# A three-layer graph network on one core: batch turns three tiles apart, sums in two buffers, edge weights ahead of z, edges begun one tile later

## The reference, cut to what matters

```
def gat_conv(x, src, dst, W, att_src, att_dst, bias, n):      # layers 1 and 2
    h = x @ W
    e = leaky_relu((h @ att_src)[src] + (h @ att_dst)[dst], 0.2)
    e = exp(e - segment_max(e, dst, n)[dst])
    alpha = e / segment_sum(e, dst, n)[dst]
    return segment_sum(alpha[:, None] * h[src], dst, n) + bias

def gcn_conv(x, W, b, src, dst, n):                           # layers 3 and 4
    h = x @ W
    norm = dinv[src] * dinv[dst]                              # dinv = 1/sqrt(degree)
    return segment_sum(h[src] * norm[:, None], dst, n) + b

h  = relu(layernorm(x))
x1 = x + gat_conv(relu(gat_conv(h, ...)), ...)                # src, dst with a self-loop per node
h  = relu(layernorm(x1))
out = x1 + gcn_conv(relu(gcn_conv(h, ...)), ...)
```

## Time and profile before

| | us |
|---|---|
| runs | 2162.92, 2172.12, 2168.01 |
| median | 2168.01 |
| profiled execution | 2162.72 |
| its span, first to last instruction | 2160.5 |
| TensorE busy | 2103.2 (97%) |
| VectorE busy | 1418.8 (66%) |
| ScalarE busy | 951.1 (44%) |
| POOL busy | 851.6 (39%) |
| granted TensorE clock, mean | 0.991 |

### The profile page before, as it was taken

How to read it: one execution, slowest core, us unless ns; L and a number is a source line. 1 busy time by engine, 2 the same in 40 slices (tenths; PEclk the granted TensorE clock), 3 DMA queues, 4 the chain that set the end, 5 groups by cost and what they waited for, 6 DMA issues and landing times.

```text
span 2160.5 us, 34890 instructions
## 1 busy us (share of the span) xinstructions
PE 2103.2 (97%) x12917; PEld 1312.5 (61%) x12917; DVE 1418.8 (66%) x3186; ACT 951.1 (44%) x1328; POOL 851.6 (39%) x1067
## 2 busy tenths in 40 slices
PE   7999999999999999999998999999998999999997
PEld 4666666556666666666665556666665666656664
DVE  8989754435776675435897888565466547876652
ACT  4444454434554554444554454333333343334442
POOL 3221167614332321344544443443344422336552
PEclk9999999999999999999999999999999999999999
DMA  5998899994555559998786443576797626776552
GB/s 185 237 223 200 229 216 195 214 233 161 192 176 196 197 180 245 230 219 217 261 282 214 166 161 132 165 248 223 265 318 281 226 103 213 245 223 215 196 193 93
DMA packets 297486, 451.94 MB, mean 209 GB/s; under 512 B 193267, under 2 KB 193465, under 8 KB 297190
## 3 DMA queue, kind: packets, MB, share of 16 engines
q1 hardware_dynamic: 256950, 277.12, 46.0%
q0 software_dynamic: 40368, 172.60, 25.5%
HBM read 234.94 MB, written 179.89 MB: 192 GB/s over the span
## 4 chain that ended last, share of the span: by engine, by line
PE 86%; DVE 6%; DMA 3%; ACT 2%; issue 2%; POOL 1%; SPq 0%; POOLq 0%; ACTq 0%; DVEq 0%
PE ps_h L1077 67%; PE ps_h L1096 9%; PE ps_z L1040 4%; PE ps_e L1175 1%; PE ps_e L1176 1%; PE ps_e L1165 1%; PE ps_e L1166 1%; DMA rows<-e_out 1%; DVE edge_mem L1393 1%; DVE bn L1264 1%; DVE x_keep L1290 0%; DVE x_keep L1286 0%; DMA edge_mem<-meta_rows 0%; DMA out<-res,perm_out 0%; DVE res L1382 0%
## 5 line engine op out<-in xcount | busy, mean ns | idle before, releaser
L1077 PE MATMUL ps_h<-w_hi,x_keep 128*128 128x384 f16 x2568 | 526.4, 326 | 1.1 <-issue 1.1
L1077 PE MATMUL ps_h<-w_hi,z_hi 128*128 128x384 f16 x1572 | 388.0, 329 | 1.5 <-DVE w_lo L1254 1.5
L1077 PE MATMUL ps_h<-w_lo,z_hi 128*128 128x384 f16 x1572 | 387.4, 328 | 0.0
L1077 PE MATMUL ps_h<-w_hi,z_lo 128*128 128x384 f16 x1572 | 386.4, 328 | 0.0
L1077 PEld LDWEIGHTS ps_h<-w_hi,x_keep 128*128 128x128 f16 x2568 | 249.9, 98 | 164.7 <-issue 2.4
L1077 PE MATMUL ps_h<-w_lo,x_keep 128*128 128x384 f16 x1284 | 313.7, 326 | 0.0
L903 ACT ACTIVATE row_out<-ps_h,grow 128x768 f32<-128x768 f32 x159 | 142.9, 899 | 366.8 <-PE ps_h L1077 365.9
L1330 DVE TENSOR_TENSOR z_lo<-ps_z,z_hi 128x768 f16<-128x768 f32 x131 | 125.0, 954 | 155.5 <-ACT z_hi L916 155.4
L734 POOL TENSOR_SCALAR veps<-mv 128x1 f32<-128x1 f32 x158 | 43.8, 277 | 458.0 <-DVE mv L1267 455.5
L1361 DVE TENSOR_TENSOR res<-z,res 128x768 f16<-128x768 f32 x107 | 102.3, 956 | 183.7 <-ACT res L949 94.3
L1077 PEld LDWEIGHTS ps_h<-w_lo,z_hi 128*128 128x128 f16 x1572 | 154.9, 99 | 104.1 <-issue 3.6
(11 more groups left out here) (252 smaller groups left out, 3609.9 us busy)
## 6 DMA issues: line engine op xcount, KB each, us to landing
rows<-row_out SPq DMA_DIRECT2D x199, 384.0 KB, 3.8
rows<-e_out SPq DMA_DIRECT2D x60, 384.0 KB, 4.6
row_in<-in_x SPq DMA_DIRECT2D x40, 384.0 KB, 4.3
row_in<-rows SPq DMA_DIRECT2D x40, 384.0 KB, 5.1
x_rows<-pre SPq DMA_DIRECT2D x40, 384.0 KB, 3.7
res<-x_rows SPq DMA_DIRECT2D x40, 384.0 KB, 4.4
pure_rows<-row_out SPq DMA_DIRECT2D x39, 384.0 KB, 2.6
row_in<-pure_rows SPq DMA_DIRECT2D x39, 384.0 KB, 4.9
```

The costliest lines, as they stand in the source:

```text
L1077: last = nc.tensor.matmul(ps_h[s][:, a, 0:HALF], zp[:, c, :], wp[:, c, a * HALF:(a + 1) * HALF], start=(c == 0 and zp is zh and wp is hi), ...
```

## The change

Four edits:

1. The three tiles of a batch that follows plain tiles (the first of each part: places 178, 248 and 286) are turned three places apart, at g - 7, g - 4 and g - 1 instead of g - 3, g - 2 and g - 1. In the other batches nothing changes.
2. The plain sums of layer 3 are written to two buffers by turns (`e_tmp` and `e_out`, as `last_out`), each with a semaphore of its own for its store; VectorE waits for the store before the last one. SP issues the store at the start of its window instead of at its end.
3. On ScalarE, `weights` comes before `make_z` instead of after it, in all score tiles of both layers.
4. The edges of layer 2 begin at place 161 instead of 160, the plain sums at 233 instead of 232. Their first gathers on POOL stay (`edge_rows(layer, 0)` at place 159) or move with them (the plain sums').

```diff
     def put_batch():
         b, g = count[0], len(seq)
         count[0] += 1
-        follows = b > 0 and seq[g - 1].chain
-        last = [t.g for t in seq if t.chain and t.layer == 4][-THREE:]
-        turns = [last[0], last[1], g - 1] if last and b > 0 and last[1] >= g - 12 else [g - 3, g - 2, g - 1]
+        apart = 1 if seq[g - 1].chain else 3
+        turns = [g - 1 - 2 * apart, g - 1 - apart, g - 1]
...
-    EDGES = {1: begin["2"] + 2, 2: begin["3"] + 2}
-    plain_at = {begin["4"] + 4 + (7 * j) // 5: j for j in range(ET)}
+    EDGES = {1: begin["2"] + 2, 2: begin["3"] + 3}
+    plain_at = {begin["4"] + 5 + (7 * j) // 5: j for j in range(ET)}
...
             def edge_store(layer, h, j):
-                if layer in GATS:
-                    sp.wait_ge(e_out_ready, h + 1)
-                else:
-                    sp.wait_ge(edge_done, h + 3)
+                sp.wait_ge(e_out_ready, h + 1)
                 sp.dma_start(table_tile(layer, NT + j), e_out[:, :]).then_inc(e_stored, 16)
+
+            def plain_store(j):
+                sp.wait_ge(edge_done, 2 * ET + j + 3)
+                sp.dma_start(table_tile(3, NT + j), last_out[j % 2]).then_inc(plain_stored[j % 2], 16)
...
+                if w - 1 in plain_at:
+                    plain_store(plain_at[w - 1])
                 t = tile(w, -1)
                 if t and t.stored:
                     store(t)
...
-                if w - 1 in plain_at:
-                    j = plain_at[w - 1]
-                    edge_store(3, j + 2 * ET, j)
...
                     if t.mixed and t.pos == FREE:
-                        pool.wait_ge(e_stored, 16 * ((t.layer - 1) * ET + 1))
+                        if t.layer == 4:
+                            for s in range(2):
+                                pool.wait_ge(plain_stored[s], (ET + 1 - s) // 2 * 16)
+                        else:
+                            pool.wait_ge(e_stored, 16 * ((t.layer - 1) * ET + 1))
...
                 for t in turned[:1]:
                     upper_parts(t)
+                if gat and not first and now is not None:
+                    weights(now + h0)
                 for t in due(w + 1):
                     make_z(t)
...
                     divide(before + h0)
-                if gat and not first and now is not None:
-                    weights(now + h0)
...
                 else:
-                    dve.wait_ge(e_stored, (h + 1) * 16)
-                    base = last_base[j % 4]
-                    V.tensor_tensor(e_out[:, 0:SPLIT], base[:, 0:SPLIT], e_lo, ALU.add)
-                    V.tensor_tensor(e_out[:, SPLIT:D], base[:, SPLIT:D], ps_e[:, 1, 0:D - SPLIT], ALU.add).then_inc(edge_done, 1)
+                    if j < 2:
+                        dve.wait_ge(e_stored, (2 * ET + 1) * 16)
+                    else:
+                        dve.wait_ge(plain_stored[j % 2], (j // 2) * 16)
+                    base, to = last_base[j % 4], last_out[j % 2]
+                    V.tensor_tensor(to[:, 0:SPLIT], base[:, 0:SPLIT], e_lo, ALU.add)
+                    V.tensor_tensor(to[:, SPLIT:D], base[:, SPLIT:D], ps_e[:, 1, 0:D - SPLIT], ALU.add).then_inc(edge_done, 1)
```

More of the change, by code:

```diff
@@ L501, in build @@
         e_stored = sem("e_stored")
+        plain_stored = [sem(f"plain_stored{s}") for s in range(2)]
         base_stored = [sem(f"base_stored{s}") for s in range(3)]
```

## The result

The changed kernel takes 2176.51 us in the median of 18 runs (2171.10 to 2182.19), the kernel before, on the same chips, 2167.38 (18 runs, 2160.36 to 2172.12). The ratio is 1.0044 with a 95% interval of 1.0035 to 1.0054: 9.5 us slower, between 7.6 and 11.7. The forecast was 2170.2 us, +2.2. The profiled execution took 2178.17 us, its span is 2176.0.

A forecast was written before the change was run, and what follows sets the result against it. TensorE, busy 97% of the span, was taken as the bound, so only its waits and lower clock could change; the terms summed to +2.2 us, put on the median of 2168.0: 2170.2 us, range 2155 to 2183.

The forecast's parts named there:

- E: Places 244 to 246: two sum buffers and turns three tiles apart would take 9.9 us off an excess of 10.4.
- F: Places 283 and 284: turns three tiles apart would take 3.3 us off an excess of 5.4.
- C: Four batches from place 178: edges from 161 make stripe 2 and product 1 late score tiles, +16.1 us.
- B: Places 173 to 176, before the first batch: spread turns find no room on VectorE, +3.6 us on 10.9.
- D: Place 234: two buffers for the third layer's sums would remove its whole excess, -2.8 us.
- A: Places 161 and 162, where the second layer's edges begin: starting one tile later takes 1.5 us off 4.7.
- Rival 1: VectorE's idle time absorbs the parity, so B and C would be 0: 2150.5 us, faster; chance 0.17.
- Rival 2: Lateness is carried from batch to batch, with four clock drops: sum +14.6, 2182.6 us, slower; chance 0.15.
- Rival 3: The sums' store did not hold E; its wait goes to the batch's low half: E -3, 2177 us; chance 0.06.

The follow-up runs named there:

- e3: The changed kernel with z put back ahead of the weights on ScalarE, edges still from place 161: 2178.32 us, ratio 1.0035 to the kernel before.
- e5: e4 with the turns three tiles apart in the first batch of the first part only: 2162.33 us, ratio 0.9979 to the kernel before.
- e9: e4 with the edges of layer 2 begun at place 161 instead of 160: 2177.60 us, ratio 1.0033 to the kernel before.
- e4: The kernel before with only the two buffers for the third layer's sums and SP's earlier issue of their store: 2159.40 us, ratio 0.9954.
- e1: The changed kernel with the edges of layer 2 begun at place 160 again: 2168.88 us, ratio 0.9985 to the kernel before.
- e2: The changed kernel with the edges of layer 2 begun at place 162: 2167.48 us, ratio 0.9988 to the kernel before.
- e8: e4 with turns three apart before the middle part only and the carried row ahead of the batch tile's z: 2153.88 us, ratio 0.9935.
- e7: e6 with POOL's factors for that batch's tiles computed after the next place's gather: 2152.37 us, ratio 0.9937 to the kernel before.
- e10: e4 with the weights ahead of z on ScalarE, edges from place 160: 2161.48 us, ratio 0.9960 to the kernel before.
- e6: e4 with the turns three apart before the last part only (before place 286): 2156.13 us, ratio 0.9946 to the kernel before.

## Why the prediction was right, and where not

The forecast of no change within 0.5% held; the size was 7 us short. In the traces the terms together miss by 8.9, of which E and F are 8.4. By its steps:

1. **C, parity: right.** +14.6 for +16.1. Stripe 2 was put at 1.8 us, measured 1.8 in each batch; product 1 at 3.2, measured 3.0 at a full clock (3.6 in the two batches where the clock fell within the place); two clock drops of four were put at 3.4, and two came, of 1.6 and 1.4 with the 0.6 that falls into product 1. Inside, one term was wrong: 0.8 us of each wait was laid on z behind the weights. With z first (e3), z waits for POOL's factors and the weights for z, and stripe 2 still has 1.9 and product 1 2.6 at a full clock: z behind the weights is worth nothing at the one and 0.4 at the other, and the rest belongs to the parity. VectorE's chain was put at 1.0 and 2.4, so at stripe 2 it was too short by as much as z was too long. That the sum came out there is luck.
2. **B: near in the sum, partly by luck.** Waits were put at 3.5 in place 170, 4.9 at the end of 171, and 1.3 + 2.2 in 174, the clock at 1.6 after 171 and about 1 for another drop; excesses of 3.2 (170), 5.1 (171), 1.7 (172), 3.9 (174) and 1.5 (175) came. But TensorE stood only 2.7, 3.2 and 1.1 + 2.2, and the clock fell three times: it is 0.88 in place 171, 0.80 in 172 and 0.84 in 175, which costs 1.6 + 1.7 + 1.5. The waits were put 2.7 too long and the clock some 2 too cheap. The prediction laid the rise on the spread turns alone (+3.6). Alone they make +5.0 (e5), the parity alone +4.3 (e9), both +5.2: the two do not add here (that they fill the same idle time of VectorE was not shown), and the term was some 1.6 small.
3. **D, two buffers: right**, -2.8 (e4), with the earlier issue in it.
4. **E: wrong by 3.9 us.** The -9.9 was to come from buffers and spread turns together. The buffers alone bring -8.3 (e4), and the changed kernel then has 2.3 more: place 240 has an excess of 3.8, the rest of E 0.6. 1.7 of the 3.8 is the clock; in e1, with the same wait of 1.89, it stays at 1.00, place 240 has 2.1 and E 2.7. In the four kernels with the same code here (it, e1, e2, e3) E is between 2.7 and 5.1. The sums also begin one place later in all four, and no run has that start alone, or these turns in this order without it. The failed step is "A batch tile's two loads move with it": it moved the loads, but not the batch tile's z on ScalarE, which waits for POOL's factors and now stands ahead of a carried row; with the row ahead of z, 0.6 is left (e8).
5. **F: wrong by 4.5 us, and in sign.** The same step ends in "the eviction that needs it comes two tiles, 13 us, later: 0". It followed SP's queue and asked only for the store; on POOL, factors and gather share one queue, and the rows of a plain tile came 1.3 and 2.1 us late. VectorE's balance (4.05 us over three places) was right: e7, which takes POOL's order away, leaves 1.8 where 2.2 were forecast. How late the rows come varies: in the four kernels with the changed kernel's order (it, e1, e2, e3) F is between 5.7 and 9.3.
6. **A: right**, -1.1 for -1.5.

Rival 1, that VectorE's idle time absorbs the parity, is refuted by e1 and e9. The share that it argued from even fell: VectorE was busy for 37.73 of 43.99 us of a batch and is for 38.65 of 48.32 now, 80% after 86, while TensorE waits more for it. The Trainium skill's "Perfetto Trace Analysis", section "Identifying the Most-Contended Engine", takes VectorE's occupancy as a fair measure of how close it is to roofline. It does not say that an engine with time to spare is never late; that reading, which the prediction gave as the page's, does not hold here. The work between an edge part and the next score is serial, and its lateness does not show in the share. Rival 2, lateness carried on, is refuted by the changed kernel's trace: the waits at product 1 are 2.6 us in the first batch and 2.5 in the three others, and two drops came, not four. Rival 3 is refuted by e4: E loses 8.3 with no turn moved.

The net of 9.5 us therefore comes from four edits. One gains (buffers with the earlier store, -10 us by e4), one loses more (edges at an odd place, +17 by e9), and one does next to nothing (weights before z, e3 and e10). The spread turns lose 5.0 in the first place by e5, where VectorE has no room, and 2.3 in the second, with the sums' later start in it; in the third, 0.6 (e6) is less than F varies from kernel to kernel. Added up, -10, +17, +5.0, +2.3 and +0.6 make 15: some 4 of it is counted twice, since in B the parity and the spread turns do not add. When the carried row and the gather go first, the spread turns gain 1.5 in the second place (e8) and 3.7 in the third (e7).

## What to carry to other kernels

An order that alternates with period two against a pattern of six has a phase; shift one against the other and a different step meets the longest chain, so the start place is a parameter to be tried at both parities. When a step is moved, write down its instruction on every engine, not only its loads: here the losses that the prediction missed came from a z and a gather that it had not counted. A second buffer and an earlier issue took away a wait on a store with no loss seen elsewhere; apply such an edit by itself, and each half of it by itself, before those that trade one wait for another.

## What the runs showed that was not expected

Layer 1, the same in all these kernels, had 2.9 us of excess in the profiled execution of before, and between 6.8 and 13.2 in the other twelve, mostly in places 61 to 70. The stretch in the changed kernel, and in the one before:

```profile
395.00:460.00 65.00, 59.02 (x351) 34.34 (x349) 27.82 (x66) 27.78 (x30) 26.90 (x49) 0.97 1.16 228
```
```profile
394.00:459.00 65.00, 61.21 (x375) 36.23 (x374) 30.01 (x69) 28.79 (x33) 28.29 (x52) 1.00 1.16 224
```

The share of the DMA engines is 1.16 in both, and in the same 65 us TensorE does 351 matmuls in the one and 375 in the other; which transfer comes late each time stays open. So single profiled spans differ by up to 10 us in a stretch that no edit touches, and the profile of before has the lowest value of the thirteen. That is about as much as the 5.3 us by which it lay under its median; that it is the reason was not shown. Spans should be compared without such a stretch, or by many runs.

Whether the clock drops after a wait is not certain from its length alone: after waits of some 2.5 us in all at product 1 it fell in two batches of the changed kernel (0.87 and 0.90 in the next tile) and stayed at 1.00 in the two others; in e3 and in e9, after 2.3 to 2.4 us, it fell in three of four. A drop there is worth 1.4 to 1.7 us, so C can differ by that much with the same waits.
